# A first gather layer whose one-hot comparisons read their row of numbers, and their edge weights, from PSUM bank 3

## The reference, cut to what matters

```python
def _L0_gnn_ref(features, src, dst, W_src, gamma, beta):
    feat_src = features @ W_src
    msgs = feat_src[src]                                  # 100000 gathered rows
    sums = segment_sum(msgs, dst, num_segments=n)
    deg = segment_sum(ones, dst, num_segments=n)
    x = sums / maximum(deg, 1.0)[:, None] + features
    x = (x - mean(x, 0)) * rsqrt(var(x, 0) + BN_EPS) * gamma + beta
    return relu(x)

def _L1_gnn_ref(h6_all, edge_index, edge_weight, ...):    # the third layer
    row, col = edge_index                                 # row = src, col = dst
    deg = segment_sum(edge_weight, row) + 1               # weighted, by source
    ...

x = x + _L0_gnn_ref(_layernorm(x), src, dst, ...)
x = x + _L0_ffn_ref(_layernorm(x), ...)                   # 8 experts, one per row
x = x + _L1_gnn_ref(_layernorm(x), [src, dst], edge_weight, ...)
x = x + _L1_ffn_ref(_layernorm(x), ...)                   # 8 experts, two per row
```

## Time and profile before

| | |
|---|---|
| median of 3 timed runs | 3881.25 us (3871.81 to 3883.53) |
| span of the profiled execution, first to last instruction | 3460.0 us |
| median less that span | 421.25 us |
| busy, share of the span: PE, DVE, ACT, POOL | 82%, 69%, 38%, 65% |
| granted TensorE clock, mean over the span | 0.916 |
| first gather layer, first gather to last | 114.5 to 1234.3 us, 830 gathers |
| gathers of the third layer | 1920.7 to 2962.0 us, 830 gathers |

### The profile page before, as it was taken

One profiled execution on the slowest core, in us unless ns is written; L12 is line 12 of the kernel. 1 busy time (PEld: TensorE's weight loads), 2 busy tenths in 40 slices (PEclk: granted clock), 3 DMA queues, 4 the chain that ended last, 5 costly groups with the idle time before them and its releaser, 6 DMA issues.

```text
span 3460.0 us, 49772 instructions
## 1 busy us (share of the span) xinstructions
PE 2823.5 (82%) x13479; PEld 2074.6 (60%) x13479; DVE 2398.5 (69%) x6173; ACT 1316.1 (38%) x3306; POOL 2240.4 (65%) x2178
## 2 busy tenths in 40 slices
PE   5777776888888878998899777777777777699999
PEld 4444443666666665665788354445444444589998
DVE  5687798888888876665577566766766676554443
ACT  4444566777777553442111111111111111245554
POOL 1677777777777754400566677777777777256666
PEclk9899889999999989998999788887888888799999
DMA  5333333333333335542566444444444444433443
GB/s 169 98 102 101 98 96 101 103 99 103 101 103 101 103 98 152 153 142 90 174 197 204 121 136 136 138 135 136 136 145 135 136 135 124 74 60 62 68 67 59
DMA packets 209833, 405.71 MB, mean 117 GB/s; under 512 B 48262, under 2 KB 131807, under 8 KB 209297
## 3 DMA queue, kind: packets, MB, share of 16 engines
q0 software_dynamic: 124624, 303.07, 33.6%
q1 hardware_dynamic: 78736, 93.04, 8.1%
q10 hardware_dynamic: 6192, 6.29, 0.6%
HBM read 316.98 MB, written 88.96 MB: 117 GB/s over the span
## 4 chain that ended last, share of the span: by engine, by line
PE 57%; issue 13%; DVE 11%; POOL 11%; DMA 4%; ACT 4%; DVEq 1%; POOLq 0%; ACTq 0%
PE bank L784 15%; POOL ring_or_weights L798 10%; PE bank L2240 6%; PE bank L1829 6%; PE bank L2249 6%; PE bank L1547 5%; PE bank L1318 4%; PE bank L1117 3%; DMA ring_or_weights<-scaled_and_whole_rows,item_other_node 3%; PE bank L1038 3%; DVE acc_or_weights L744 3%; PE bank L1562 2%; PE bank L1991 2%; ACT normed L1024 1%; DVE normed L729 1%
## 5 line engine op out<-in xcount | busy, mean ns | idle before, releaser
L798 POOL DMA_INDIRECT ring_or_weights<-gather_table,item_other_node x830 | 865.4, 1043 | 269.4 <-issue 226.6
L744 DVE TENSOR_TENSOR acc_or_weights<-bank,acc_or_weights 128x257 f32 (+1 forms) x1660 | 701.3, 422 | 384.6 <-PE bank L784 346.9
L798 POOL DMA_INDIRECT ring_or_weights<-scaled_and_whole_rows,item_other_node x830 | 789.7, 951 | 255.3 <-issue 236.1
L784 PE MATMUL bank<-ring_or_weights 128*128 128x256 f32 x1660 | 616.3, 493 | 267.5 <-DVE acc_or_weights L744 126.4
L784 PE MATMUL bank<-ring_or_weights,normed 128*128 128x257 f32 x1660 | 525.3, 411 | 154.7 <-issue 124.7
L784 PEld LDWEIGHTS bank<-ring_or_weights 128*128 128x128 f32 x1660 | 333.0, 234 | 507.4 <-issue 360.0
L784 PEld LDWEIGHTS bank<-ring_or_weights,normed 128*128 128x128 f32 x1660 | 279.7, 196 | 305.6 <-issue 265.7
L1117 PE MATMUL bank<-acc_or_weights,normed 128*98 128x256 f32 x782 | 251.2, 403 | 90.8 <-ACT acc_or_weights L1105 86.7
L736 DVE TENSOR_SCALAR ring_or_weights<-iota_row,item_local_node,item_weight 128x128 f32<-128x128 f32 x830 | 296.5, 357 | 6.0 <-issue 5.9
L1100 ACT ACTIVATE acc_or_weights<-iota_row,ring_or_weights 128x128 f32<-128x128 f32 x782 | 285.9, 391 | 7.0
L1024 ACT ACTIVATE normed<-normed,edge_records_by_src 128x64 f32<-128x64 f32 x784 | 209.1, 341 | 176.5 <-DVE normed L999 173.5
(11 more groups left out here) (357 smaller groups left out, 4534.5 us busy)
## 6 DMA issues: line engine op xcount, KB each, us to landing
hidden_rows<-normed SPq DMA_DIRECT2D x49, 512.0 KB, 2.6
ring_or_weights<-gather_table,item_other_node POOLq DMA_INDIRECT x830, 2.8
ring_or_weights<-scaled_and_whole_rows,item_other_node POOLq DMA_INDIRECT x830, 2.8
acc_or_weights<-in_L_ffn_Wd SPq DMA_DIRECT2D x8, 1024.0 KB, 5.9
acc_or_weights<-in_L_ffn_W SPq DMA_DIRECT2D x16, 512.0 KB, 6.9
gather_table<-normed SPq DMA_DIRECT2D x7, 896.0 KB, 4.1
hidden_rows<-x_rows SPq DMA_DIRECT2D x7, 896.0 KB
gather_table<-normed SPq DMA_DIRECT2D x24, 258.0 KB, 3.4
```

What stands on the lines that cost most here:

```text
L744: v.tensor_tensor(into, bank[i % nbank][:, 0:width], into, ALU.add).then_inc(added, 1)
L784: m.matmul(bank[i % nbank][:, 0:width], lhsT=hot, rhs=ring[:, i % RING, 0:width], start=True, stop=True).then_inc(sum_made, 1)
L798: g.indirect_dma_start(ring[:, i % RING, 0:D], None, table, IndirectOffsetOnAxis(ap=gidx[:, i:i + 1], axis=0)).then_inc(ring_in[i % RING], 16)
```

## The change

The row of numbers is copied once, at the start of the layer, from SBUF into the first 128 columns of PSUM bank 3. The comparisons of lines 729, 809, 990 and 999 read it there. The edge weights of line 811 are copied into the next columns of bank 3, for 47 groups of 8 edge columns at a time, three times in the layer. Bank 3 is no longer there for item sums, so the layer's main loop runs over banks 0 to 2. Line 1005 still reads its two inputs from SBUF, and so does line 948. The arithmetic is the same.

```diff
+    FIRST_BANKS = 3
+    numbers = bank[3][:, 0:P]
+    WBATCH = 47
+    near_weight = bank[3][:, P:P + WBATCH * HOTS]
@@ one_hots
-        v.tensor_tensor(hot1[:, at:at + n, :], iota[:, :].unsqueeze(1).broadcast_to([P, n, P]),
+        v.tensor_tensor(hot1[:, at:at + n, :], numbers.unsqueeze(1).broadcast_to([P, n, P]),
                         dloc[:, b * HOTS:b * HOTS + n].unsqueeze(2).broadcast_to([P, n, P]),
                         ALU.is_equal).then_inc(hots_in, 1)
@@ tile_hots
+        at = b % WBATCH * HOTS
+        if at == 0:
+            some = min(WBATCH * HOTS, EC - b * HOTS)
+            v.tensor_copy(near_weight[:, 0:some], rec1[:, b * HOTS:b * HOTS + some, 1])
-        vs.then(v.tensor_tensor(hot, iota[:, 0:T].unsqueeze(1).broadcast_to([P, n, T]),
+        vs.then(v.tensor_tensor(hot, numbers[:, 0:T].unsqueeze(1).broadcast_to([P, n, T]),
                                 kt1[:, cols].unsqueeze(2).broadcast_to([P, n, T]), ALU.is_equal))
-        v.tensor_tensor(hot, hot, rec1[:, cols, 1].unsqueeze(2).broadcast_to([P, n, T]), ALU.mult).then_inc(hi_done, 1)
+        v.tensor_tensor(hot, hot, near_weight[:, at:at + n].unsqueeze(2).broadcast_to([P, n, T]), ALU.mult).then_inc(hi_done, 1)
@@ spread_rows
-        v.tensor_tensor(row_hot[:, b % 2, 0:n, :], iota[:, :].unsqueeze(1).broadcast_to([P, n, P]),
+        v.tensor_tensor(row_hot[:, b % 2, 0:n, :], numbers.unsqueeze(1).broadcast_to([P, n, P]),
@@ spread_lanes
-        v.tensor_tensor(lane[:, 0:n, :], iota[:, 0:LO].unsqueeze(1).broadcast_to([P, n, LO]),
+        v.tensor_tensor(lane[:, 0:n, :], numbers[:, 0:LO].unsqueeze(1).broadcast_to([P, n, LO]),
@@ first_vector
+        vs.then(v.tensor_copy(numbers, iota[:, :]))
         tile_hots(0)
-        aggregate_vector(0, AW, 4, beside_first_vector)
+        aggregate_vector(0, AW, FIRST_BANKS, beside_first_vector)
@@ first_tensor
-        aggregate_tensor(0, AW, 4, beside_first_tensor)
+        aggregate_tensor(0, AW, FIRST_BANKS, beside_first_tensor)
```

## The result

| | before | the change |
|---|---|---|
| median | 3887.68 us (3871.81 to 3922.28, 14 runs) | 3913.08 us (3902.64 to 3931.37, 14 runs) |
| ratio | | 1.0058, 95% interval 1.0039 to 1.0076 |

The prediction was 3834 us, faster. The profiled execution of the changed kernel has a span of 3900.9 us and took 3902.64 us, so a run takes 1.7 us beside its span. The prediction put 421 us there.

The account below looks back on a forecast made before the run. GpSimd was taken to pace the first gather layer, whose savings the kernel would keep in full. Gains of 7.9 + 4.5 + 7.5 + 28 less 1 gave 46.9, rounded to 47: 3881.25 - 47 = 3834 us, range 3808 to 3868.

Parts of the forecast that it names:

- GpSimd paces this layer: First gather layer: GpSimd hardly waits for a free slot, so its long gathers are the reserve, 79.7 us.
- 201 to 321: Stretch from 376 to 540 us, ring of slots full at times: 7.5 us gain, between nothing and 11.4.
- -1 (copies): Four added copies to PSUM, 1.5 us together, taken as a cost of 1 us.
- Why a gather is long: First layer: gathers run long where VectorE reads two SBUF operands, 1.96 us against 0.95 beside one SBUF operand.
- The prediction's signs: Gathers' mean falls from 1043 to some 960 ns; those still long start inside lines 1013, 956 or their like.
- The operand in PSUM at no cost: Five changed VectorE lines: reading one operand from a bank costs 0, as line 744 takes 420 ns.
- rival of a dearer column: PSUM broadcast reads 25% dearer a column: 62 us of VectorE, some 25 us slower, 3906 us; chance 0.08.
- 65 ns an instruction: Rival: dearer start for 534 PSUM-reading instructions in the big stretch, 35 us on VectorE; about 3872 us, chance 0.11.
- Three banks at 0: Item sums: TensorE three items ahead of the adds instead of four costs 0, with 17 us as other end.
- The big stretch at 28: 600 to 1200 us, 438 gathers: gain 28 us, between the loop's 24.6 and 47 if GpSimd still paced.
- the rival in which GpSimd paces to the end: Waits at line 990 shrink with the gathers, so the big stretch gains 47 us: 3812 us, chance 0.16.
- the bank: Rival: with one bank fewer for sums, 17 us of gain come off where the ring is full; 3851 us, chance 0.08.

Follow-up runs that it names:

- the spaced kernel: Kernel before plus a 128-column GpSimd memset behind each gather of the first layer: 0.9988 of before, 3889.07 us.
- long chip: A chip, or a session's state, on which the kernel before took 3854.91, 3894.17 or 3887.87 us in its session.
- chip 13: Session in which before took 3458.63 us; the plain change ran at 0.9854 of it, 3407.60 us.
- chip 2: Session in which before took 3854.91 us; the change, run again, was at 1.0044 of it, 3870.88 us.
- quick chip: A chip, or a session's state, on which the kernel before took 3459.23 or 3458.63 us in its session.
- Three banks alone: Kernel before with three banks for the first layer's item sums, comparisons and weights still read from SBUF: 0.9978 and 1.0001 of before.
- with four banks: The change with four banks for item sums, numbers and weights in bank 4, then from item 300 in bank 6: 1.0017 and 1.0044 of before.
- the spaced change: The change plus a 128-column GpSimd memset behind each gather of the first layer: 1.0017 of before, 3895.57 us.

## Why the prediction was wrong, step by step

**The step that failed** is the sentence "its span is 3460.0 us; the median of the timed runs is 421.25 us above it, and I take that difference as unchanged", with "GpSimd paces this layer" built on the same span. The 421 us do not lie beside the span. They lie inside it, mostly in the two gather layers, where hand-overs between the engines come late. All 19 profiled executions of the result and the experiments have spans within 2 us of their times, and before takes either some 3459 us or 3855 and more; so the profile and the timed runs of before were of two kinds, though no record names the chip of either. On the kind that was timed, GpSimd is not the pace-setter (the spaced kernel, 0.9988): it stands idle for 421 us before the change and for 495 and 511 after it, some 250 of each being the 0.30 us between gathers. Why a long chip's hand-overs are late stays open.

**The terms of the sum**, by the same gathers (us from gather 1 to 159, to 201, and so on; before in its first profile and the change on chip 13; and both on chip 2):

| stage | predicted gain | quick chip | chip 2 |
|---|---|---|---|
| gathers 1 to 158 | 7.9 | 205.6 - 198.2 = 7.4 | 228.0 - 229.0 = -1.0 |
| 159 to 200, 322 to 368 | 4.5 | 117.3 - 112.4 = 4.9 | 133.5 - 138.0 = -4.5 |
| 201 to 321 | 7.5 | 165.5 - 156.1 = 9.4 | 187.5 - 190.7 = -3.2 |
| 369 to 806 | 28 | 602.3 - 568.6 = 33.7 | 685.7 - 682.9 = 2.8 |
| rest | -1 (copies) | 29.1 - 29.2 = -0.1 | 33.1 - 33.2 = -0.1 |
| sum | 47 | 55.3, and 51.0 by the medians | -6.0 |

The quick chip's profile, by the stretches of the earlier trace rows:

```profile
L802 POOL DMA_INDIRECT ring_or_weights<-gather_table,item_other_node x158 | 150.1, 950 | 60.2 <-issue 37.5 <-DMA gather_table<-normed 12.4 <-PE bank L788 10.4
L802 POOL DMA_INDIRECT ring_or_weights<-gather_table,item_other_node x42 | 40.2, 958 | 12.8 <-issue 11.6 <-PE bank L788 1.2
L802 POOL DMA_INDIRECT ring_or_weights<-gather_table,item_other_node x121 | 116.9, 966 | 39.2 <-issue 33.5 <-PE bank L788 5.7
L802 POOL DMA_INDIRECT ring_or_weights<-gather_table,item_other_node x47 | 45.0, 958 | 14.3 <-issue 11.3 <-PE bank L788 3.1
L802 POOL DMA_INDIRECT ring_or_weights<-gather_table,item_other_node x438 | 418.6, 956 | 150.0 <-issue 113.9 <-PE bank L788 36.2
```

- *Why a gather is long*: right on both kinds of chip. The prediction's signs came: the mean fell to 956 and 957 ns, and what is long starts beside lines 1013 and 956. Beside the changed line 990 (998 now) a gather is of normal length on chip 13:

```profile
772.67 0.68 DVE L998 TENSOR_TENSOR normed<-bank,edge_positions 128x512 f32<-128x512 f32 x1
772.75 0.94 POOL L802 DMA_INDIRECT ring_or_weights<-gather_table,item_other_node  x1 [0.52 <-issue]
```

  The rule of the Trainium skill ("SBUF — State Buffer", "Who interferes with whom"), that two SBUF inputs contend with GpSimd's reads and one does not, agrees with this: the longest gather falls from 1960 to 1222 ns. Its report that tensor_tensor leaves DMAs from GpSimd alone does not hold for this one.
- *The operand in PSUM at no cost*: right in duration. The rival of a dearer column, at 25%, is out, and so are 65 ns an instruction. (By the prediction's own sums that price gives 3869 to 3872 us, not the 3865 that it names beside the skill's figure.)
- *Three banks at 0*: right (0.9978 and 1.0001).
- *The big stretch at 28*: somewhat low, 33.7 on the quick chip. I had taken the 44.2 us of waits at line 990 as fixed. Over the layer they fell from 48.2 to 23.6 us, so the loop had some slack; the rival in which GpSimd paces to the end (47) was too high. The last stretch has 24 gathers, not 28; its term was nothing and stays so.

```profile
L998 DVE TENSOR_TENSOR normed<-bank,edge_positions 128x512 f32<-128x512 f32 x195 | 133.5, 685 | 23.6 <-PE bank L1046 23.2
```

- *The rivals* covered the operand, the bank and the loop, and none of them the profile itself. I had looked at a span of 3460.0 beside timed runs of 3881.25, and explained away what should have been the first rival: that the timed executions are not the profiled one, and that another engine paces in them. With that case at even odds the forecast would have been no change to 0.4% slower or 47 us faster, and the range would have held the result's 3913 only if it reached 0.8% above before.

**What stays open.** On long chips the change costs 0.2 to 0.6%: 1.0058, 1.0044, and with four banks 1.0017 and 1.0044. Three of the four intervals leave out 1. Three banks alone cost nothing (0.9978 and 1.0001), and TensorE's longer waits for the adds come with them, so the bank by itself isn't it. Whether it is the closer spacing of the gathers (C) or the reads from PSUM (D) isn't told: the spaced change is at 1.0017 (0.9985 to 1.0050), between what both expected.

## What to carry to other kernels

Compare the profiled span with the timed median before anything is built on the profile. If they differ by much more than the 1.7 us that lay around each span here, the timed executions may have another critical path, and the engine that "paces" in the profile may be one that waits in them. A gain on the engine that sets the pace counts in full only until something else paces, so price the change for both; here something else did from the start on three chips of five.

## What the runs showed of the hardware that I had not expected

- The same program takes 3459 us on two chips and 3855 to 3894 on three, at the same instruction durations (TensorE's apart, by its clock) and the same memory traffic (317 MB read, 89 MB written). Each chip had one session, so it could also be a state of the session.
- On the long chips the records themselves are thinner. The trace of before holds 50,838 semaphore updates in its first profile and 24,638 on chip 2, for the same 49,772 instructions. The two stages that record most lose most and stretch most:

| stage of before | records a us, quick | updates kept, chip 2 | length, quick to chip 2 |
|---|---|---|---|
| first gather layer | 44.9 | 7663 of 18871 | 1119.8 to 1267.8 us |
| between the layers | 34.3 | 5783 of 7674 | 686.4 to 718.0 |
| third layer | 42.8 | 6251 of 18118 | 1041.3 to 1242.0 |
| after it | 36.2 | 3863 of 4976 | 498.0 to 495.2 |

  (Records: instructions, updates and landings of DMAs.) That is also where "remote" and much of "issue" come from on these chips: a releaser whose record is missing. The Trainium skill, "NOTIFIC — the notification-queue block", section 7.1 on overflow, says that a record queue that is full drops records or holds up the engine that writes them, by its mode, and that the block's inner pipeline always holds up. Lost records and late hand-overs in the same stages agree with that, and then the long chips' extra time would be a cost of recording. No run here shows it, and the two gather layers are also those with the most hand-overs, so late hand-overs of any cause would stretch them most. Each timed run has a span and a granted clock too, so none is known to be free of records, and no kernel with fewer records was tried.
- Instruction fetches are not what holds the engines up: on chip 2, 5% of VectorE's restarts after more than 1.5 us of standing still have a fetch landing in the 1.5 us before them, where 6 to 13% would by chance (the fetches' times shifted by 3 to 20 us).
- The stands recur in part at the same place of the program: of 163 over 1.5 us on VectorE on chip 2 that the quick profile does not have before the same instruction, 72 are in the next kernel's profile on that chip too.
